# A decoder megakernel: the order of work at three places (geometry's transposed maxima, the scan's gate, inputs and norms, products at the end of the int8 stage)

## The chip, the cores and the metric

The kernel runs on one core of one Trainium2 chip. The metric is the device time of the whole launch in microseconds. Engines are named as the profile names them: PE is TensorE (PEld its weight loads), DVE VectorE, ACT ScalarE, POOL GpSimd, SP SyncE, which issues the DMAs.

## The reference, cut to what matters

Twelve layers follow each other, each in the form `x = layernorm(x + layer(x))`, on an input of 8 batches of 256 tokens of 256 values, in float32. Three of them are touched.

Layer 0, an attention with 16 heads whose keys and values get a part that a geometric memory has gated:

```
L = p1[_PI] * p2[_PJ] - p1[_PJ] * p2[_PI];  L / norm(L)      # lines of four projections
k_enh = k + kv_gate * gram_gate * k_geo
v_enh = v + kv_gate * gram_gate * v_geo
scores = einsum('bhtd,bhsd->bhts', q, k_enh) * SCALE         # causal
out = softmax(scores) @ v_enh;  out @ out_w + out_b
```

Layer 8, a product of numbers rounded to int8:

```
q_lhs = clip(round(lhs / lhs_scale), -127, 127)   # lhs_scale: absmax of a row / 127
q_rhs = clip(round(rhs / rhs_scale), -127, 127)
return (q_lhs @ q_rhs) * lhs_scale * rhs_scale
```

Layer 9, a gated selective scan with 512 channels and 16 states:

```
gate = sigmoid(x @ W_gate.T + b_gate)
x_proj, delta_proj = split(x @ W_in.T + b_in);  delta = relu(delta_proj)
h = h * exp(A * d_t[..., None]) + (x_t * d_t)[..., None] * B_mat      # over 256 tokens
y_t = h @ c0
return gate * (y + x_proj * D_vec) @ W_out.T + b_out
```

## The kernel before

Each layer is a stage, a function that writes an instruction list for each engine by hand. There is no scheduler: what stands first in an engine's list runs first, and the engines meet at semaphores that count upwards (`M.max_done`, `M.prod_done` and so on). PSUM is eight banks: `R` (four), `T` (two) and `O` (two).

**geometry16 (layer 0).** The loop runs over rounds i = -2 to 11; batches pass through it in a pipeline, so that round i holds the scores of batch i (`scores`, queries by keys, L1624 and L1628, three parts f = 0, 1, 2), the scores by key of batch i-1 (`scores_t`, L1651, L1656), its products with the values (L1673, L1677), older outputs, and the features of batch i+2 (`features`, transposes, L1586). VectorE takes from the scores the negated maxima of the rows (`maxima`, `neg_max`, L1939). TensorE transposes these (`maxima_transposed`, L1637) into the bank `S_y`, ScalarE copies them to `neg_t` (L1836), and SyncE's DMA (L1495) writes them into a row of `q_pad`, so that `scores_t` of the same batch, in the next round, subtracts the maximum inside its product. `scores` and `scores_t` use the four banks of `R` in turn: a part is written when the maxima or the exponentials (L1832) before have been read. The bank `S_y` is shared, in the order of the table `MIXED_JOBS`, by the features, the maxima (`neg`), the memory (`mem`, L1595) and others; `mixed_free` waits until the job before has been read out. The three features of a round are read out by VectorE (`scanned`, L1907 a scan over tokens, L1910 a product). `maxima_transposed(i)` stands at the end of round i, behind `features(i, 2)`, and `scores(i + 1, 0)` begins the next. The rounds that have features are -2 to 5; `neg` is there in rounds 0 to 7, so that six rounds have both. The text counts these as first to sixth.

**int8_product (layer 8).** VectorE quantises rows of batch i, TensorE transposes them (L2993) and multiplies (L3003), VectorE adds the residual and normalises batch i-3 (L3099), TensorE transposes the result (`transposed`, L3013) for the next stage and ScalarE copies it to `x_t` (L3051). `keep_warm` (L212) is a 128x512 product into a part of PSUM that nothing reads; it stands once in each round but the last four, which have no rows left to transpose.

**selective_scan (layer 9).** The work is cut into 16 units i: four pairs of batches g, each with four blocks of 128 channels ct. A unit has 16 states n. ScalarE computes the decays (L3349, into a ring of 6), VectorE scans (`scanned`, L3418, into a ring of 10), TensorE adds two states at a time into `R` (`summed`, L3255). For the next unit TensorE projects `delta`, `x` and gate (L3224) and ScalarE reads them (L3335, L3339 to `xp`, L3343); VectorE forms `u = xp * delta` (`weighted`, L3411). When a unit's sums are complete, ScalarE copies the odd half (`odd`), TensorE adds it swapped (`swapped`, L3261), VectorE multiplies with the gate (`product`, L3424), and TensorE projects the output (`output`, L3276). After the fourth block of a pair, in the first unit of the next pair (`leaving`, three such units), VectorE adds the residual and takes statistics (`residual`, L3429), GpSimd computes the reciprocal deviation (`rstd`, L3490 and L3492), VectorE normalises (`normalised`, L3442), TensorE transposes (`transposed`, L3285) and ScalarE copies (L3364), for each of the pair's two batches. The numbers n in the code say behind which scan, pair of sums or decay each of these stands.

## Time and profile before

| | us |
|---|---|
| the three runs | 3420.35, 3420.55, 3434.16 |
| their median | 3420.55 |
| the profiled execution | 3430.85 |
| its span, first to last instruction | 3429.0 |
| TensorE busy, 90% of the span | 3095.6 |
| VectorE busy, 48% | 1661.0 |
| ScalarE busy, 36% | 1221.8 |
| geometry's stage, from the start of the span | about 388 |
| int8's stage | about 2640 to 2682 |
| the scan's stage | about 2682 to 3038 |

The profile is of one execution, whose times are counted from its first instruction. A row of it names the engine, the line, the tile written and those read; "idle before" is the time that the engine stood still just before the row's first instruction, with what ended it. TensorE's instructions are pipelined: the next one starts before the recorded end of the one before it. The granted clock is given as a share of 2.4 GHz, so that 0.50 is the lower level of 1.2 GHz.

### The profile page before, as it was taken

Reading aid. Unit: us, or ns where it says so; the run is one execution under the profiler, and the core shown is the slowest. Engines: PE = TensorE matmul, PEld = TensorE weight load, DVE = VectorE, ACT = ScalarE, POOL = GpSimd, SP = SyncE. Lnnn points to the kernel's source line nnn. Section 1 sums busy time; section 2 is a strip of 40 time slices with the busy share of each in tenths; the row PEclk is TensorE's granted clock in tenths of the full one; section 3 lists DMA queues with packets and bytes.
Section 4 is the critical chain, followed back from the end, with each engine's and each line's share of the span. In section 5 each row is a group of like instructions: output and inputs, shape, how many; then the busy total and the mean of one; then the engine's idle time right before and its main releaser. Section 6 shows DMA issues by size and latency. Waiting matters only on the chain. (4 is left out here: it accounts for less than half of the span.)

```text
span 3429.0 us, 56123 instructions
## 1 busy us (share of the span) xinstructions
PE 3095.6 (90%) x22948; PEld 1968.3 (57%) x22948; DVE 1661.0 (48%) x2939; ACT 1221.8 (36%) x2636; POOL 291.0 (8%) x511
## 2 busy tenths in 40 slices
PE   6999899999989998899999988989998888889695
PEld 4565466666658886656666655656555333346363
DVE  4565344444433323634444443225557899956112
ACT  1322254445431112234544441123332666633011
POOL 1111100000000000000000000000111000001202
PEclk9999999999999999899999999989999999989897
DMA  2001000000100002000000000010000000000332
GB/s 103 18 13 61 9 1 1 1 1 1 59 16 0 0 0 79 20 1 1 1 1 1 1 26 28 12 33 21 10 28 34 16 1 1 1 19 14 148 129 85
DMA packets 36410, 85.14 MB, mean 25 GB/s; under 512 B 3246, under 2 KB 30103, under 8 KB 32599
## 3 DMA queue, kind: packets, MB, share of 16 engines
q1 hardware_dynamic: 31831, 75.06, 6.3%
q0 software_dynamic: 1536, 4.20, 0.4%
q8 instruction: 170, 2.79, 0.3%
q10 hardware_dynamic: 2816, 2.62, 0.2%
q14 instruction: 57, 0.47, 0.0%
HBM read 53.90 MB, written 9.44 MB: 18 GB/s over the span
## 5 line engine op out<-in xcount | busy, mean ns | idle before, releaser
L2329 ACT ACTIVATE prob<-R,neg_max 128x333 f32<-128x333 f32 x512 | 268.6, 538 | 183.1 <-DVE neg_max L2399 183.1
L3418 DVE TENSOR_TENSOR_SCAN arena<-arena,u 128x512 f32<-128x512 f32 x256 | 289.6, 1204 | 0.1
L2399 DVE TENSOR_REDUCE neg_max<-R 128x2 f32<-128x666 f32 x256 | 205.6, 845 | 98.1 <-PE R L2209 98.1
L2220 PEld LDWEIGHTS T<-const,prob 128*128 128x128 f32 (+1 forms) x1536 | 183.6, 143 | 96.2 <-issue 66.1
L2405 DVE COPY prob_t<-T 128x384 f32<-128x384 f32 x256 | 141.7, 553 | 189.0 <-PE T L2220 183.8
L2220 PE MATMUL T<-const,prob 128*128 128x128 f32 (+1 forms) x1536 | 210.5, 273 | 19.7 <-DVE prob_t L2405 19.5
L2336 ACT ACTIVATE prob_t<-T 128x384 f32<-128x384 f32 x256 | 126.1, 493 | 213.9 <-PE T L2220 207.2
L3349 ACT ACTIVATE arena<-delta,neg_a 128x510 f32<-128x510 f32 x256 | 176.5, 714 | 53.4 <-DVE arena L3418 52.7
L2169 PE MATMUL O<-arena,keys_in 128*128 128x512 f32 (+1 forms) x384 | 183.8, 603 | 5.0 <-ACT arena L2310 2.4
L2164 PE MATMUL O<-keys_in,arena 128*128 128x333 f32 x512 | 170.3, 458 | 1.2 <-DVE arena L2380 1.2
L3255 PE MATMUL R<-arena,diag 64*64 64x512 f32 x1024 | 138.6, 635 | 33.2 <-DVE arena L3418 32.9
L2648 PE MATMUL R<-x_t,arena 128*128 (+1 forms) x640 | 152.1, 382 | 1.0 <-PEq L2644 0.6
L2512 POOL COPY rec_rows<-rec 128x256 f32<-128x256 f32 x128 | 51.2, 400 | 1001.5 <-DVE rec L2410 1001.5
L2648 PEld LDWEIGHTS R<-x_t,arena 128*128 128x128 f32 x640 | 121.7, 191 | 20.1 <-issue 3.2
L2158 PE MATMUL O<-keys_in,arena 128*128 128x256 f32 x512 | 124.4, 387 | 3.2 <-ACT keys_in L2304 2.4
L2657 PE MATMUL O<-arena,hid 128*128 128x256 f32 x512 | 121.3, 380 | 2.3 <-PEq L2654 2.3
L2180 PE MATMUL O<-arena,attn_t 128*128 128x256 f32 x512 | 117.4, 382 | 1.0 <-DVE ysb L2382 1.0
L2770 DVE SCALAR_TENSOR_TENSOR ysb<-O,gate_b,ysb 128x256 f32<-128x256 f32 x112 | 49.1, 480 | 142.8 <-DVEq L2767 142.8
L2416 DVE TENSOR_TENSOR attn_t<-O,arena 128x256 f32<-128x256 f32 x128 | 53.8, 420 | 130.4 <-ACT arena L2341 130.4
L2164 PEld LDWEIGHTS O<-keys_in,arena 128*128 128x128 f32 x512 | 88.1, 190 | 40.9 <-DVE arena L2380 7.4
L2657 PEld LDWEIGHTS O<-arena,hid 128*128 128x128 f32 x512 | 97.1, 190 | 16.0 <-issue 2.6
L2158 PEld LDWEIGHTS O<-keys_in,arena 128*128 128x128 f32 x512 | 92.2, 189 | 22.0 <-ACT q_t L2307 4.2
(463 smaller groups left out, 5497.0 us busy)
## 6 DMA issues: line engine op xcount, KB each, us to landing
w<-w_dram SPq DMA_DIRECT2D x16, 1024.0 KB, 7.5
arena<-pack_dram SPq DMA_DIRECT2D x2, 4100.0 KB, 15.0
q_pad<-q_pad SPq DMA_DIRECT2D x24, 224.0 KB, 2.7
arena<-pack_dram SPq DMA_DIRECT2D x4, 1284.0 KB, 6.0
arena<-pack_dram SPq DMA_DIRECT2D x1, 4896.0 KB, 15.1
arena<-k_nat SPq DMA_DIRECT2D x16, 224.0 KB, 2.7
arena<-arena SPq DMA_DIRECT2D x16, 224.0 KB, 2.9
arena<-pack_dram SPq DMA_DIRECT2D x1, 2707.0 KB, 14.9
```

The costliest lines, as they stand in the source:

```text
L2158: last = nc.tensor.matmul(bank[:, h * T:(h + 1) * T], wq[:, c, (2 * i + h) * P:(2 * i + h + 1) * P], keys[:, c, CTX:XK], start=(c == 0), s ...
L2164: last = nc.tensor.matmul(bank[:, 0:XK], wkv[:, c, i * P:(i + 1) * P], keys[:, c, :], start=(c == 0), stop=(c == C - 1))
L2169: last = nc.tensor.matmul(bank[0:n, :], keys[:, c, first:first + n], wkv[:, c, XI + i % 2 * BANK:XI + (i % 2 + 1) * BANK], start=(c == 0), ...
L2220: last = nc.tensor.transpose(S.T[0:n, i, kc * P:(kc + 1) * P], prob[:, g % 2, i, first:first + n], S.ident)
L2329: last = nc.scalar.activation(prob[:, g % 2, i, :], S.R[:, g % 2, i * BANK:i * BANK + XK], ACT.Exp, bias=neg_max[:, g % 2, i:i + 1], accum ...
L2399: nc.vector.tensor_reduce(neg_max[:, g % 2, :], S.R[:, g % 2, :].rearrange("p (i n) -> p i n", i=2)[:, :, 0:XK], AX.X, ALU.max, negate=Tru ...
L2405: nc.vector.tensor_copy(prob_t[:, m % 2, 0, :, qt * P:(qt + 1) * P], S.T[:, 0, 0:3 * P].rearrange("p (c q) -> p c q", c=3)).then_inc(M.pt_ ...
L2648: last = nc.tensor.matmul(S.R[:, e % 2, f * T:(f + 1) * T], w[:, f * P:(f + 1) * P], S.x_t[:, c, bass.ds(b * T, T)], start=(c == 0), stop= ...
L2657: last = nc.tensor.matmul(S.O[:, slot, tt * D:(tt + 1) * D], src[:, f * T + tt * P:f * T + (tt + 1) * P], w[:, f, :], start=(f == 0), stop ...
L3255: last = nc.tensor.matmul(sums(i, a)[to:to + HB, :], diag[rows, i % CT, n + a, :], state[rows, (q + a) % HELD, :], start=(a == 1 and n == ...
L3349: nc.scalar.activation(decay[:, q % DEEP, :].rearrange("p (b t) -> p b t", b=PAIR)[:, :, 1:T], delta[:, i % 2, :].rearrange("p (b t) -> p ...
L3418: nc.vector.tensor_tensor_scan(state[:, q % HELD, :], decay[:, q % DEEP, :], u[:, i % 2, :], 0.0, ALU.mult, ALU.add)\
```

## The change

- geometry: `maxima_transposed(i)` goes from the end of round i to the next round, behind `scores(i + 1, 0)`. `neg_max` gets two copies that alternate by batch.
- int8: each of the last three rounds gets one unread product (L212) ahead of its transposes.
- scan, VectorE: the product with the gate goes from behind scan 6 to behind scan 7, `weighted` from 8 to 9, the first residual from 11 to 12, the first norm and the second residual from 13 to 15, and the second norm from 15 to scan 2 of the next unit. TensorE: the transposes of the second batch go from behind the first pair of sums to behind the third. ScalarE: their copy goes from decay 8 to decay 12.

```diff
@@ geometry16
-        neg_max = sb("neg_max", [P, TT, H])
+        neg_max = sb("neg_max", [P, 2, TT, H])
...
                 if now:
                     scores(i, 0)
+                if before:
+                    maxima_transposed(i - 1)
                 written(i, 0)
...
                 features(i, 2)
-                if now:
-                    maxima_transposed(i)
...
@@ int8_product, tensor
                     keep_warm(nc, S, unread, 1)
+                if i >= B:
+                    keep_warm(nc, S, unread, 1)
                 if 0 <= i - 3 < B:
                     transposed(i - 3)
...
@@ selective_scan, tensor
                     summed(i, n)
+                    if n == 4 and g >= 1 and ct == 1:
+                        transposed(PAIR * g - 1)
                     if n == 0:
-                        if g >= 1 and ct == 1:
-                            transposed(PAIR * g - 1)
                         if i + 1 < UNITS:
                             deltas(i + 1)
...
@@ selective_scan, scalar
-                    if n == 8 and g >= 1 and ct == 1:
+                    if n == 12 and g >= 1 and ct == 1:
                         transposed(PAIR * g - 1)
...
@@ selective_scan, vector
-                    if n == 6 and i >= 1:
+                    if n == 7 and i >= 1:
                         product(i - 1)
-                    if n == 8 and i + 1 < UNITS:
+                    if n == 9 and i + 1 < UNITS:
                         weighted(i + 1)
-                    if n == 11 and leaving:
+                    if n == 12 and leaving:
                         residual(PAIR * g - 2)
-                    if n == 13 and leaving:
+                    if n == 15 and leaving:
                         normalised(PAIR * g - 2)
                         residual(PAIR * g - 1)
-                    if n == 15 and leaving:
+                    if n == 2 and g >= 1 and ct == 1:
                         normalised(PAIR * g - 1)
```

TensorE's list between round 0 and round 1 of geometry: L1637 transposes the maxima, L1624 and L1628 are the scores of the next batch, L1535 the first projection of its round.

```order
@@ -52,7 +52,7 @@
 L1573 MATMUL T<-arena,x_t 128x512 x2
 L1586 MATMUL T<-const,arena 112x128 x4
-L1637 MATMUL T<-const,neg_max 16x128 x2
 L1624 MATMUL R<-k_pad,q_pad 128x128 x16
 L1628 MATMUL R<-masks,ident_b 128x512 x4
+L1637 MATMUL T<-const,neg_max 16x128 x2
 L1535 MATMUL T<-arena,x_t 128x192 x2
 L1538 MATMUL T<-arena,x_t 128x192 x2
```

The transposed maxima went behind the 20 products of the next scores; nothing else changed its place.

VectorE's list in the scan, from the residual of the first leaving unit to the gate product of the unit behind it, before. L3418 are the scans.

```order
L3429 TENSOR_TENSOR ysb_own<-O,x_nat 128x512
L3433 BN_STATS bst<-ysb_own 128x6 x2
L3436 BN_AGGR mv<-bst 128x2 x2
L3418 SCALAR_TENSOR_TENSOR arena<-arena,u 128x512 x2
L3442 TENSOR_SCALAR x_nat<-ysb_own,mv,rstd 128x256 x2
L3429 TENSOR_TENSOR ysb_own<-O,x_nat 128x512
L3433 BN_STATS bst<-ysb_own 128x6 x2
L3436 BN_AGGR mv<-bst 128x2 x2
L3418 SCALAR_TENSOR_TENSOR arena<-arena,u 128x512 x2
L3442 TENSOR_SCALAR x_nat<-ysb_own,mv,rstd 128x256 x2
L3418 SCALAR_TENSOR_TENSOR arena<-arena,u 128x512 x7
L3424 SCALAR_TENSOR_TENSOR gated<-gated,R 128x512
```

The same piece of VectorE's list after the change. The lines of this stage are two further down in the changed file, so that L3420 are the scans and L3426 the gate product.

```order
L3431 TENSOR_TENSOR ysb_own<-O,x_nat 128x512
L3435 BN_STATS bst<-ysb_own 128x6 x2
L3438 BN_AGGR mv<-bst 128x2 x2
L3420 SCALAR_TENSOR_TENSOR arena<-arena,u 128x512 x3
L3444 TENSOR_SCALAR x_nat<-ysb_own,mv,rstd 128x256 x2
L3431 TENSOR_TENSOR ysb_own<-O,x_nat 128x512
L3435 BN_STATS bst<-ysb_own 128x6 x2
L3438 BN_AGGR mv<-bst 128x2 x2
L3420 SCALAR_TENSOR_TENSOR arena<-arena,u 128x512 x3
L3444 TENSOR_SCALAR x_nat<-ysb_own,mv,rstd 128x256 x2
L3420 SCALAR_TENSOR_TENSOR arena<-arena,u 128x512 x5
L3426 SCALAR_TENSOR_TENSOR gated<-gated,R 128x512
```

Three scans stand between each statistics and its norm where there were two; the boundary of the units, which lay behind the second norm, now lies behind the second statistics.

## Rows read from the trace of the kernel before

**Rows 1.** Which engine is busy in the scan stage: stretch, then its length, busy us, clock, DMA.

```profile
2682.00:3038.00 356.00, 310.22 (x1472) 109.63 (x1472) 327.89 (x355) 224.74 (x378) 16.87 (x16) 0.93 0.01 4
```

**Rows 2.** Time order, geometry, end of a round: start, us, engine, line, shapes, idle before.

```profile
207.87 0.60 PE L1586 MATMUL T<-const,arena 128*112 128x128 f32 x4
...
209.84 0.38 PE L1637 MATMUL T<-const,neg_max 128*16 128x128 f32 x2 [1.36 <-DVE arena L1910]
...
210.14 1.17 PE L1624 MATMUL R<-k_pad,q_pad 16*128 16x128 f32 x32
...
210.25 0.37 ACT L1836 ACTIVATE neg_t<-T 16x256 f32<-16x256 f32 x1 [1.58 <-PE T L1637]
...
212.12 0.82 PE L1535 MATMUL T<-arena,x_t 128*128 128x192 f32 x4
```

**Rows 3.** Time order, TensorE, the same place in the fifth and sixth round.

```profile
248.72 0.38 PE L1637 MATMUL T<-const,neg_max 128*16 128x128 f32 x2 [1.72 <-DVE arena L1910]
...
288.88 0.38 PE L1637 MATMUL T<-const,neg_max 128*16 128x128 f32 x2 [1.37 <-DVE arena L1910]
```

**Rows 4.** Busy time by stretch, behind two of those gaps (columns as in rows 1).

```profile
133.00:136.00 3.00, 3.00 (x40) 2.11 (x39) 0.18 (x1) 0.37 (x1) 0.00 (x0) 0.77 0.04 11
...
136.00:139.00 3.00, 3.00 (x39) 2.64 (x41) 2.11 (x1) 0.49 (x1) 0.00 (x0) 0.66 0.00 0
...
252.00:255.00 3.00, 3.00 (x43) 2.56 (x45) 1.85 (x1) 0.49 (x1) 0.00 (x0) 0.65 0.00 0
```

**Rows 5.** Time order, TensorE: scores by key, sixth round and eighth.

```profile
294.58 1.15 PE L1651 MATMUL R<-q_pad,k_pad 17*128 17x256 f32 x16
...
355.89 1.15 PE L1651 MATMUL R<-q_pad,k_pad 17*128 17x256 f32 x16 [0.22 <-DMA q_pad<-neg_t]
```

**Rows 6.** Instructions of tile neg_t: its DMA, duration ns min/median/max, first and last start.

```profile
L1495 SPq DMA_DIRECT2D q_pad<-neg_t x8: 572/594/698, 99.0 to 354.0; - x8
```

**Rows 7.** Time order, TensorE, end of int8 and the scan's first projections.

```profile
2673.03 1.02 PE L212 MATMUL R<-ctx_t,const 128*128 128x512 f32 x2
...
2680.30 0.66 PE L3013 MATMUL R<-const,x_nat 128*128 128x128 f32 x4 [0.46 <-DVE x_nat L3099]
...
2682.07 8.24 PE L3224 MATMUL T<-x_t,arena 128*128 128x512 f32 x12 [1.11 <-PEq L2962]
```

**Rows 8.** Busy time by stretch, before the scan stage (columns as in rows 1).

```profile
2681.00:2681.50 0.50, 0.00 (x0) 0.00 (x0) 0.00 (x0) 0.50 (x1) 0.00 (x0) 0.50 0.00 0
```

**Rows 9.** Time order, scan: the first xp on ScalarE, a projection on TensorE at 1.00.

```profile
2688.63 0.69 ACT L3339 ACTIVATE xp<-T,arena 128x512 f32<-128x512 f32 x1 [2.08 <-PE T L3224]
...
2798.68 1.88 PE L3224 MATMUL T<-x_t,arena 128*128 128x512 f32 x4
```

**Rows 10.** Time order, VectorE in the scan stage, where it idles.

```profile
2689.42 0.69 DVE L3411 TENSOR_TENSOR u<-xp,delta 128x512 f32<-128x512 f32 x1 [4.36 <-ACT xp L3339]
...
2701.54 0.69 DVE L3411 TENSOR_TENSOR u<-xp,delta 128x512 f32<-128x512 f32 x1 [1.19 <-ACT xp L3339]
...
2782.61 0.69 DVE L3429 TENSOR_TENSOR ysb_own<-O,x_nat 128x512 f32<-128x512 f32 x1 [0.57 <-PE O L3276]
...
2787.22 0.73 DVE L3442 TENSOR_SCALAR x_nat<-ysb_own,mv,rstd 128x256 f32<-128x256 f32 x2 [0.54 <-POOL rstd L3492]
...
2802.68 0.69 DVE L3424 SCALAR_TENSOR_TENSOR gated<-gated,R 128x512 f32<-128x512 f32 x1 [1.65 <-PE R L3261]
...
2806.12 15.72 DVE L3418 TENSOR_TENSOR_SCAN arena<-arena,u 128x512 f32<-128x512 f32 x14
...
2822.18 0.69 DVE L3424 SCALAR_TENSOR_TENSOR gated<-gated,R 128x512 f32<-128x512 f32 x1 [0.34 <-PE R L3261]
...
2963.18 0.74 DVE L3442 TENSOR_SCALAR x_nat<-ysb_own,mv,rstd 128x256 f32<-128x256 f32 x2 [0.55 <-POOL rstd L3492]
...
2973.36 0.69 DVE L3424 SCALAR_TENSOR_TENSOR gated<-gated,R 128x512 f32<-128x512 f32 x1 [1.62 <-PE R L3261]
```

**Rows 11.** Busy time by stretch, first leaving unit (columns as in rows 1).

```profile
2790.00:2792.00 2.00, 0.02 (x3) 0.02 (x3) 1.93 (x2) 0.76 (x2) 1.85 (x2) 0.50 0.00 0
```

More of the change, by code:

```diff
@@ L1636, in maxima_transposed @@
                 for qt in range(TT):
-                    last = nc.tensor.transpose(S_y[0:H, qt * P:(qt + 1) * P], neg_max[:, qt, :], S.ident)
+                    last = nc.tensor.transpose(S_y[0:H, qt * P:(qt + 1) * P], neg_max[:, b % 2, qt, :], S.ident)
                 last.then_inc(M.ya_full, 1)
@@ L1937, in maxima @@
                 n = P if f == 0 else T
-                neg = neg_max[:, min(f, 1), :].rearrange("p (j c) -> p j c", j=4)
+                neg = neg_max[:, b % 2, min(f, 1), :].rearrange("p (j c) -> p j c", j=4)
                 nc.vector.tensor_reduce(neg if f == 0 else neg[:, :, 2 * f - 2:2 * f],
```

## The prediction

> **What bounds the kernel now.** I read the busy time by stage first, then the order of events at the three places that the edit touches, engine by engine, and there only what ends last. The kernel as a whole is TensorE's, but the three places differ. In geometry's loop TensorE is the bound. Its queue runs dry once in each of the six rounds that carry features: behind the last four transposes of the features (L1586) stands the transpose of the maxima (L1637), which waits until VectorE has read those features out of the same PSUM bank (L1910), 1.36 us of idle time; behind L1637 stand the scores (L1624), which wait for nothing [rows 2]. In the scan stage VectorE is the bound: it is busy 327.9 of 356 us, TensorE 310.2 [rows 1], and between two VectorE instructions of a unit there is no gap but the ones that the trace names [rows 10]. At the end of the int8 stage the bound is the chain VectorE norm, TensorE transpose, ScalarE copy; behind it TensorE starts the scan's first projections at the lower of its two clock levels, 1.2 GHz (granted clock 0.50) [rows 7, 8], and the first scan waits for them.
>
> **Geometry: 8.6 us, and part of the clock.** The scores go ahead of the transposed maxima. They last 212.12 less 210.14, or 1.98 us [rows 2], longer than the 1.36 that TensorE waits, so L1637 then finds its bank read out. Five gaps of 1.36 to 1.37 and one, the fifth, of 1.72 [rows 2, 3] give 8.6. Bounds: from the start of L1586 to that of L1535 are 4.25 us, of which after the change 0.6 (L1586), 1.98 and 0.3 (L1637) are left, so 1.4 a round or 8.2 in all; if the transposes of L1586 overlap what follows as L1637 does, 1.6 a round or 9.6. What is moved back: L1637 starts about 0.5 us later on the clock, and 1.9 later against TensorE's work, and with it ScalarE's neg_t, SyncE's DMA into q_pad and the scores by key (L1651) that wait for it. ScalarE's in-order queue has neg_t at its head and waits next for L1535's product, which comes behind L1637 again, so nothing is blocked there. The DMA lands in at most 1.9 us: the last one is issued at 354.0 and L1651 starts at 355.89, after 0.22 of waiting [rows 5, 6]. The tightest feature round is the sixth, where L1651 starts at 294.58, 5.7 us behind its L1637 at 288.88 [rows 3, 5]: the path of neg_t takes 0.41 to ScalarE, 0.37 there [rows 2] and 1.9, in sum 2.7, and the room that is left is 5.7 less 1.9 less 2.7, or 1.1. So no new wait; the cost if it fails is in the rivals. L1624 now meets its own waits (the DMAs of keys and queries, the exponentials of the round before) 1.7 us earlier; in rows 2 it starts straight behind L1637, so how much earlier it could start isn't shown, and the bounds for that are nothing and the whole 8.6. In the seventh round L1637 sat in a wait for ScalarE, and afterwards it costs its own 0.3. The second copy of neg_max adds no instruction.
>
> In two of the six rounds the gap is followed by about 6 us in which the granted clock averages 0.7, that is a stretch at 1.2 GHz and the rest at 2.4 [rows 4]. Lost: (1 - 0.77 + 1 - 0.66) x 3, or 1.7 us, and as much in the other, whose second half reads 0.65. Without the gap before it the drop should be gone: 3.4 in this execution. Below nothing: a drop that comes elsewhere costs as much. Since four like gaps have none behind them, I carry half, 1.7, to other executions. The Trainium skill (TensorE: Matmul & The Clock Gate, Part 1) says that the phase of the chip's look at activity isn't tied to the kernel, so that slow matmuls differ from run to run; two of six gaps agree with that. By that rule the drops are no property of the gap alone, and the whole gain would be 1.7 us smaller.
>
> **End of int8: 2.4 us.** Three unread products are added before the last three transposes. Each is like the present ones, 1.02 us of TensorE [rows 7]. The first two fall in idle time. The third stands between the last two transposes, where TensorE has 0.46 idle: the last transpose, its copy and the end of the stage come 0.1 to 0.6 later; I take 0.3, because the next instruction starts before the recorded end of the one before it (0.86 behind the start of this product). In exchange TensorE doesn't idle for most of the 5 us before the stage's end. In the trace the clock falls to 0.50 at about 2681 [rows 8], and the first scan's input waits for eight matmuls: from 2682.07 to ScalarE's xp at 2688.63, 6.56 us. Four such matmuls take 1.88 at 2.4 GHz [rows 9], eight then 3.8, and xp is 2.7 earlier. VectorE's own setup ends 4.36 us before the product of xp starts [rows 10], so it allows that. Net 2.4. Ends: -0.3 (the clock falls all the same) and 2.7.
>
> **Scan: 12.0 us.** All of it is idle time of VectorE. (1) The product with the gate moves one scan later, n = 6 to 7. A scan is 15.72 / 14, or 1.12 us [rows 10]. In the first unit after each leaving pair it waits 1.65 (the last of the three: 1.62) for TensorE's swapped sums, in the next unit 0.34 [rows 10]. One scan would cover 1.12 of the first; the other 0.53 goes because more VectorE work now stands ahead of it: the first batch's norm (0.73) and the second's residual (0.69 and its statistics) [rows 10] come behind the last scan of the old unit, where they came before it. (2) The input product moves from n = 8 to 9: in unit 0 it waits 1.19 for xp, and 0.07 stays: 1.1. (3) Each norm now has three scans (3.36) between itself and its residual rather than two. It waited 0.54 for GpSimd after two, so 1.12 more covers it: six times 0.54. (4) The residual is one scan later and no longer waits 0.57 for the output product: three times. Sum of a leaving pair: 1.65 + 0.34 + 1.08 + 0.57 = 3.64; three of them 10.9; with (2) 12.0. Each unit's last product, outputs and norms after the last scan aren't touched.
>
> What is moved past what: TensorE's transposes of the second batch go from behind the first to behind the third pair of sums, ScalarE's copy from its decay 8 to 12. The decays run up to six scans ahead of VectorE, so the copy is wanted at about scan 7, and the output product that reuses its bank stands behind the fifth pair, which needs scan 9. A wait of ScalarE for the transposes there is covered by the decays in hand. TensorE: in the leaving unit it is busy 0.02 of the 2 us from 2790 to 2792, at a granted clock of 0.50 [rows 11]; there a norm and a residual stand between the fourteenth and the fifteenth scan. In the new order only the first residual is left among a unit's last scans, so I expect it to drop less. It has little room in the unit behind: 310.2 us over 16 units is 19.4 each [rows 1], against 16 scans of 1.12 and two products of 0.69 on VectorE, 19.3, or 20.0 with a norm.
>
> **Sum.** 8.6 - 0.3 + 3.4 + 2.4 + 12.0 = 26.1 us, or 3404.7 from the profiled execution's own 3430.85. That one is 10.3 above the median of 3420.55, beside 3434.16, and drops of the clock like the two above may be part of it. On the median I take 26.1 - 1.7 = 24.4: 3396.
>
> **Rivals.** (A) As above, 0.55. (B) The clock doesn't follow: the scan still opens at 1.2 GHz (-2.7) and the drops only move (-1.7): 3400.5; for it speaks that 1.11 us without any product stay between the stages [rows 7]; 0.15. (C) In geometry the DMA of the maxima takes the removed wait's place: it would have to land 1.1 us later than now, and takes back at most the 8.3: 3404; 0.05. (D) VectorE's pause now falls at the start of the unit in which TensorE has most to do. If its clock drops there rather than in the idle half, the three projections (1.88 each at 2.4 GHz [rows 9]) take 5.6 us longer, the swapped sums and xp are late, and three times 5.6, 17 us, come back: 3413; against it, the pauses of VectorE are spread over two units; 0.12. (E) The other side: the same, but TensorE stays at 1.2 GHz through that whole unit, 39 us against VectorE's 20.0: 3 x 19 less 24 is 33 slower, 3453. It decides once more than 8.1 us are lost in each, which is 16 us in a row at 1.2 GHz; in the trace it is back at 2.4 by 2798.68 [rows 9], 7 us after the stretch of rows 11: 0.03. (F) The executions fall where 3434.16 fell, 13.6 higher, with the gain intact: 3410; 0.10.
>
> **Numbers.** 3396 is A's, with a range of its own from 3388 to 3403 (its ends: 9.6 and 8.2 in geometry, clock 0 or 3.4, int8 0 to 2.7, 1.5 us of scan waits left). For 8 in 10 the range runs to F and D: 3387 to 3412. A change under 0.5% (17.1 us) can't be told from none here; that is above 3403.4. Faster: A nearly whole, most of B, little else: 0.70. Slower by as much: E and a piece of F: 0.04. Same: 0.26.
>
> **What would show it.** Right: L1637 without idle time before it and L1535 some 1.5 us nearer to L1586; a granted clock of 1.00 at the scan's first projections and their twelve matmuls in 5.7 rather than 8.24 us; no waits of VectorE in the units 1 to 14 for gate, rstd or output. Wrong: idle time of L1651 for its DMA; the gate product waiting in the unit behind a leaving one with TensorE at 0.50; or all three as forecast and a total that hasn't moved, which would mean that the stages between lost on the clock what these gained.

## The result

| Kernel | Median, us | Lowest to highest, us | Executions | Profiled execution, its span, us | Granted clock |
|---|---|---|---|---|---|
| before | 3420.85 | 3420.35 to 3434.16 | 4 | 3430.85, 3429.0 | 0.960 |
| changed | 3389.51 | 3381.86 to 3401.92 | 4 | 3394.49, 3392.7 | 0.967 |

The ratio of the changed kernel to the one before is 0.990, 95% interval 0.9865 to 0.9935: faster by 31 us by the medians (22 to 46 by the interval). By the ratio itself it is 34 us, or about 3387. The prediction was 24.4 us, 3396. A second comparison of the same two kernels (below) gave 0.9911, 0.9884 to 0.9938, which is 30 us. The direction and the places were right, the size was forecast too small.

To see where the time went I cut each trace at the first instruction of a stage. Stage lengths in us:

| Trace | start and geometry (layer 0) | layers 1 to 6 | layer 7 and int8 (8) | scan (9) | layers 10 and 11 |
|---|---|---|---|---|---|
| before | 388.5 | 2111.5 | 182.1 | 356.3 | 390.6 |
| changed | 373.1 | 2107.2 | 182.2 | 339.4 | 390.8 |
| difference | -15.4 | -4.3 | +0.1 | -16.9 | +0.2 |

The 4.3 us in layers 1 to 6 aren't the change's: the same code took from 2096.6 to 2111.5 us there in ten traces.

From the page of the changed kernel, its span and its busy time by engine:

```profile
span 3392.7 us, 56135 instructions
PE 3077.6 (91%) x22954; PEld 1959.4 (58%) x22954; DVE 1659.0 (49%) x2939; ACT 1222.0 (36%) x2636; POOL 291.9 (9%) x511
```

Geometry first: the changed kernel in order of time at the end of the same round as [rows 2] (start, us, engine, line, shapes, idle before and who ended it).

```profile
202.03 0.60 PE L1586 MATMUL T<-const,arena 128*112 128x128 f32 x4
...
202.56 1.17 PE L1624 MATMUL R<-k_pad,q_pad 16*128 16x128 f32 x32
...
204.54 0.38 PE L1637 MATMUL T<-const,neg_max 128*16 128x128 f32 x2
...
204.76 0.82 PE L1535 MATMUL T<-arena,x_t 128*128 128x192 f32 x4
...
204.96 0.37 ACT L1836 ACTIVATE neg_t<-T 16x256 f32<-16x256 f32 x1 [2.13 <-PE T L1637]
```

The maxima's transpose (L1637) has no idle time before it, and from the start of L1586 to that of L1535 are 2.73 us instead of 4.25. A whole round says the same. These are the four products at L1573, which the change doesn't touch and which come once in a round, in the first two of the six rounds of before:

```profile
94.32 1.98 PE L1573 MATMUL T<-arena,x_t 128*128 128x512 f32 x4 [0.35 <-DVE arena L1882]
...
129.04 1.99 PE L1573 MATMUL T<-arena,x_t 128*128 128x512 f32 x4 [0.35 <-DVE arena L1882]
```

and in the same two rounds of the changed kernel:

```profile
94.73 1.99 PE L1573 MATMUL T<-arena,x_t 128*128 128x512 f32 x4 [0.35 <-DVE arena L1882]
...
127.92 1.98 PE L1573 MATMUL T<-arena,x_t 128*128 128x512 f32 x4 [0.35 <-DVE arena L1882]
```

The round takes 33.19 us where it took 34.72, which is 1.53 less, although the wait that went was recorded as 1.37. The fifth round, whose wait was recorded as 1.72, is 1.8 shorter once its drop of the clock is taken off. The clock, in busy time by stretch (stretch, its length, busy us of PE, PEld, DVE, ACT, POOL with instructions, granted clock, DMA share, GB/s), in before:

```profile
130.00:168.00 38.00, 35.63 (x358) 22.98 (x357) 22.37 (x30) 12.03 (x17) 3.87 (x6) 0.96 0.05 14
...
278.00:310.00 32.00, 27.75 (x287) 17.52 (x285) 18.19 (x28) 8.25 (x10) 2.19 (x6) 0.89 0.03 9
310.00:340.00 30.00, 27.83 (x295) 15.38 (x295) 10.99 (x7) 7.63 (x11) 1.20 (x2) 0.94 0.40 157
```

and in the changed kernel, whose rounds come up to 11 us earlier by then:

```profile
130.00:168.00 38.00, 36.99 (x402) 23.79 (x400) 24.15 (x33) 12.63 (x19) 3.88 (x6) 1.00 0.05 14
...
278.00:310.00 32.00, 27.74 (x386) 18.46 (x388) 18.79 (x25) 9.73 (x13) 2.14 (x4) 0.95 0.22 80
310.00:340.00 30.00, 26.81 (x296) 14.98 (x284) 11.45 (x12) 6.38 (x5) 2.13 (x4) 1.00 0.18 74
```

From 94 to 278 us the clock of the changed kernel is 1.00 throughout. Before, it was 0.96 and 0.95 in two of these rounds, the drops of [rows 4].

The end of int8 and the opening of the scan, TensorE and VectorE in order of time in the changed kernel, against [rows 7, 10], and the clock against [rows 8]:

```profile
2659.43 0.66 PE L3013 MATMUL R<-const,x_nat 128*128 128x128 f32 x4 [0.37 <-DVE x_nat L3101]
...
2659.92 1.02 PE L212 MATMUL R<-ctx_t,const 128*128 128x512 f32 x2
...
2660.78 0.60 PE L3013 MATMUL R<-const,x_nat 128*128 128x128 f32 x4
...
2662.50 5.39 PE L3226 MATMUL T<-x_t,arena 128*128 128x512 f32 x12 [1.11 <-PEq L2962]
...
2667.01 0.69 DVE L3413 TENSOR_TENSOR u<-xp,delta 128x512 f32<-128x512 f32 x1 [1.50 <-ACT xp L3341]
```

```profile
2661.00:2661.50 0.50, 0.39 (x4) 0.14 (x2) 0.00 (x0) 0.08 (x1) 0.00 (x0) 1.00 0.00 0
```

The twelve projections take 5.39 us where they took 8.24, and VectorE waits 1.50 us for xp where it waited 4.36.

The scan stage against [rows 1], and all that VectorE still waits for in it beyond the opening, 0.12 us for xp in unit 0 and 0.42 us of issue at 2928.15, against [rows 10]:

```profile
2662.00:3001.00 339.00, 301.95 (x1472) 107.52 (x1472) 326.12 (x355) 223.66 (x379) 16.86 (x16) 0.97 0.01 5
```

```profile
2990.20 0.69 DVE L3426 SCALAR_TENSOR_TENSOR gated<-gated,R 128x512 f32<-128x512 f32 x1 [3.80 <-PE R L3263]
2992.12 0.69 DVE L3431 TENSOR_TENSOR ysb_own<-O,x_nat 128x512 f32<-128x512 f32 x1 [1.22 <-PE O L3278]
2995.16 0.74 DVE L3444 TENSOR_SCALAR x_nat<-ysb_own,mv,rstd 128x256 f32<-128x256 f32 x2 [1.21 <-POOL rstd L3494]
2998.85 0.73 DVE L3444 TENSOR_SCALAR x_nat<-ysb_own,mv,rstd 128x256 f32<-128x256 f32 x2 [1.21 <-POOL rstd L3494]
```

VectorE has the same 355 instructions and works almost without a wait (0.12 and 0.42 us) through all sixteen units' scans; it is 96% busy where it was 92%. (From the int8 stage on, line numbers of the changed kernel are up to 2 higher.) What is left waits behind the last scan, which nothing was moved to cover.

### The profile page after: what moved, and what is told of

Read it like the earlier page. It is cut to its first block and busy times, and to the rows that moved or that the text cites. A ratio compares the mean times of both kernels' runs of the same rounds, so it can differ in the third digit from the quotient of the medians.

```text
span 3392.7 us, 56135 instructions
## 1 busy us (share of the span) xinstructions
PE 3077.6 (91%) x22954; PEld 1959.4 (58%) x22954; DVE 1659.0 (49%) x2939; ACT 1222.0 (36%) x2636; POOL 291.9 (9%) x511
## 2 busy tenths in 40 slices
DMA packets 36410, 85.14 MB, mean 25 GB/s; under 512 B 3246, under 2 KB 30103, under 8 KB 32599
## 5 line engine op out<-in xcount | busy, mean ns | idle before, releaser
L3420 DVE TENSOR_TENSOR_SCAN arena<-arena,u 128x512 f32<-128x512 f32 x256 | 289.5, 1201 | 0.1
L3257 PE MATMUL R<-arena,diag 64*64 64x512 f32 x1024 | 136.1, 622 | 24.6 <-DVE arena L3420 24.4
L2164 PEld LDWEIGHTS O<-keys_in,arena 128*128 128x128 f32 x512 | 88.2, 190 | 40.9 <-DVE arena L2380 7.4
L212 PE MATMUL R<-ctx_t,const 128*128 128x512 f32 x162 | 82.5, 639 | 29.1 <-DMA slots_in<-x_nat,to 26.4
```

The costliest lines, as they stand in the source:

```text
L2164: last = nc.tensor.matmul(bank[:, 0:XK], wkv[:, c, i * P:(i + 1) * P], keys[:, c, :], start=(c == 0), stop=(c == C - 1))
L3257: last = nc.tensor.matmul(sums(i, a)[to:to + HB, :], diag[rows, i % CT, n + a, :], state[rows, (q + a) % HELD, :], start=(a == 1 and n == ...
L3420: nc.vector.tensor_tensor_scan(state[:, q % HELD, :], decay[:, q % DEEP, :], u[:, i % 2, :], 0.0, ALU.mult, ALU.add)\
```

## The experiments

The theory: the gain is the sum of three independent pieces, each the idle time of the engine that bounds its stage, with the lower clock that followed it. The rivals: the pieces are worth something else when each stands alone; in geometry it is the clock and not the idle time that pays; in the scan one half of the moves does all. "Stretch" below is the time in geometry from the first L1573 to the start of the next stage. It leaves out the program's opening, in which the clock comes up at slightly different times.

**Geometry's part alone.**

```diff
-        neg_max = sb("neg_max", [P, TT, H])
+        neg_max = sb("neg_max", [P, 2, TT, H])
...
+                if before:
+                    maxima_transposed(i - 1)
...
-                if now:
-                    maxima_transposed(i)
```

> Geometry's part alone. Theory: the three parts are independent, and geometry's brings most of what the forecast missed: 1.5 us a round by the starts of the instructions (9.2 in six rounds, less 0.3 in the seventh) and 3 to 6 us of clock drops that go with the gaps, in sum 12 to 15 us less than before, about 3407. Rival 1 (the forecast's sum): 8.3 of gaps and half of 3.4 of clock, 10 less, about 3411. Rival 2 (luck in stages that nobody touched makes the difference): the rounds of this kernel spread as widely as those of before, over 14 us, and the geometry stage itself ends about 10 us earlier than before, not 15.

Measured: 0.9956 (0.9938 to 0.9974), or 15 us by that ratio; geometry's stage 376.7 us against 388.5, the stretch 331.3 against 343.8. This trace keeps one more drop of the clock than that of the changed kernel:

```profile
278.00:310.00 32.00, 27.74 (x301) 17.11 (x301) 17.48 (x25) 9.36 (x12) 2.13 (x4) 0.84 0.11 32
```

As an estimate, work at half the clock takes twice as long (eight of the scan's sums took 1.98 us in such a stretch and 1.09 at the full clock, somewhat less than twice), so that (1 - granted clock) times the stretch is what a drop costs. From 94 to 340 us before loses 8.6 us by this (1.5 + 1.8 + 3.5 + 1.8 in four stretches), this kernel 5.1, the changed kernel 1.6. With five gaps at 1.53 and the fifth at 1.8 (9.4 in sum) and 0.3 in the seventh round, that gives 9.4 - 0.3 + 3.5 = 12.6 here, where 12.5 was measured, and 9.4 - 0.3 + 7.0 = 16.1 for the changed kernel, where 15.8 was.

**The unread products at int8's end alone.**

```diff
+                if i >= B:
+                    keep_warm(nc, S, unread, 1)
```

> The three unread products at int8's end alone. Theory: the scan's first twelve matmuls run at 2.4 GHz (5.4 us rather than 8.2), the stage ends 0.3 us later, 2.4 us less in all, about 3418.5. Rival: the clock at the scan's opening isn't set by these products but by where the executions happen to lie: the twelve matmuls take 8.2 us again and the time is 0.3 more.

Measured: 0.9992 (0.9975 to 1.0008), which the comparison can't tell from nothing; the trace can. The twelve projections take 5.39 us, VectorE waits 1.51 instead of 4.36, the scan stage is 352.9 us instead of 356.3, and the stage before it 182.0 instead of 182.1. Of these 3.4 us only the 2.85 at the opening are the edit's. The other 0.5 lies in the three gate products behind the leaving units, which wait 1.37, 1.62 and 1.56 here instead of 1.65, 1.75 and 1.62, and the kernel with geometry's part alone, whose scan and int8 stages are those of before, shows the same (1.36, 1.61, 1.55), the first at

```profile
2783.91 0.69 DVE L3424 SCALAR_TENSOR_TENSOR gated<-gated,R 128x512 f32<-128x512 f32 x1 [1.36 <-PE R L3261]
```

The rival, that the opening's clock is a matter of where an execution happens to lie, falls over all traces: in the six kernels without these products (before, geometry's part, the filled gaps, the scan's part and each of its halves) the granted clock of the scan's first 5.4 us is 0.50 to 0.58, in the four with two or three of them 1.00.

**The scan's moves alone.**

```diff
+                    if n == 4 and g >= 1 and ct == 1:
+                        transposed(PAIR * g - 1)
...
-                    if n == 6 and i >= 1:
+                    if n == 7 and i >= 1:
                         product(i - 1)
-                    if n == 8 and i + 1 < UNITS:
+                    if n == 9 and i + 1 < UNITS:
                         weighted(i + 1)
-                    if n == 11 and leaving:
+                    if n == 12 and leaving:
...
-                    if n == 13 and leaving:
+                    if n == 15 and leaving:
...
-                    if n == 15 and leaving:
+                    if n == 2 and g >= 1 and ct == 1:
                         normalised(PAIR * g - 1)
```

> The scan's moves alone (gate product, input product, residuals, norms, the transposes behind them). Theory: every wait of VectorE between units goes, each worth its recorded idle time and about 0.08 us more that the next instruction gains by starting before the end of the one before it: 12.0 and 1.5 to 2, in sum 13.5 to 14 less, about 3407; the first twelve matmuls still take 8.2 us. Rival (the forecast's sum): 12.0 less, 3409.

Measured: 0.9961 (0.9943 to 0.9979), 13 us. The scan stage is 342.9 us, 13.4 less; geometry's 389.0 and the last two layers' 390.6 are as before. Of all the waits of [rows 10] the opening (4.44) is left, and beside it one of 0.68 for the gate, late in the stage, which the whole change doesn't show, and those behind the last scan.

**The whole change again,** beside its parts on the same chip.

> The whole change once more, beside its parts. Theory: the sum of the three parts, 28 to 31 us less than before, about 3391, with a spread of some 10 to 20 us between executions. Rival: the parts interact (the int8 part worth more or less once the scan is changed, or clock drops that the earlier start moves elsewhere), and the whole differs from the sum by more than 5 us.

Measured: 0.9911 (0.9884 to 0.9938), 30 us by the ratio. The three parts give 0.44%, 0.08% and 0.39%, together 0.91% against 0.89%. So they add as far as the intervals, each about 0.2% to either side, can tell. Geometry's stretch is 331.3 us here, as in the kernel with geometry's part alone, and the scan stage 339.4.

**Geometry's gaps filled, order as before.** Two unread products stand ahead of the maxima's transpose in the six feature rounds. TensorE starts them when its queue would have gone idle, and no idle time is won.

```diff
+                if now and i < B - AHEAD:
+                    if i == 0:
+                        pe.wait_ge(M.max_done, 3)
+                    else:
+                        pe.wait_ge(M.exp_done, 3 * i)
+                    keep_warm(nc, S, bank(0), 2)
                 if now:
                     maxima_transposed(i)
```

> Geometry in its old order, with two unread 128x512 products of 0.86 us each in front of the transposed maxima in the six rounds that have the gap. They fill the gap but win none of it: what this kernel gains is the clock's share alone. Theory (the removed gaps bring 9 us by themselves and about 3 by clock drops that go with them): the granted clock of the feature rounds is 1.00 throughout and the time is 3.4 to 6 less for that, 1.2 more for the products being a little longer than the gap, so 2 to 5 less than before, about 3418. Rival (the drops come from elsewhere and only happened to follow two of the gaps): they are still there in one or two rounds, and the time is 1 us more than before.

Measured: 0.9976 (0.9958 to 0.9994), 8 us by the ratio. Its stage length, 378.8, looks as good as the reorder's, but 4 us of that lie before the first round. In order of time on TensorE, the first L1573 stands at 40.5 us where before has it at 44.7: ahead of it some groups of products ran at half the pace in before and not in this execution (four of 512 columns at 31.69 took 3.78 us, here at 28.98 they took 1.99), though the edit touches nothing there. The stretch is what counts: 338.3 us, 5.5 less than before, against 12.5 less for the reorder. At the end of a round TensorE shows

```profile
202.58 0.60 PE L1586 MATMUL T<-const,arena 128*112 128x128 f32 x4
203.02 1.88 PE L212 MATMUL R<-ctx_t,const 128*128 128x512 f32 x4
204.74 0.38 PE L1637 MATMUL T<-const,neg_max 128*16 128x128 f32 x2
```

The gap has become work of 1.88 us. L1637 follows L1586 by 2.16 us where before had 1.97 (209.84 less 207.87 in [rows 2]), so a round pays 0.2 us more, about 1.2 in six. The clock is the changed kernel's:

```profile
130.00:168.00 38.00, 37.00 (x385) 23.21 (x378) 22.76 (x30) 12.02 (x17) 3.86 (x6) 1.00 0.05 14
...
278.00:310.00 32.00, 28.59 (x333) 18.23 (x333) 19.63 (x29) 8.07 (x12) 2.13 (x4) 0.95 0.03 9
310.00:340.00 30.00, 26.72 (x284) 14.82 (x286) 12.73 (x11) 6.37 (x5) 2.13 (x4) 1.00 0.37 149
```

Lost to the clock: 1.6 us instead of 8.6, so 7.0 - 1.2 = 5.8 against the 5.5 measured. This takes geometry's gain apart: 3.5 to 7 us are the clock, and the gaps themselves are the other 9. Of the 7.0 here 3.4 are the drops behind the second and the fifth gap of before. The rest lies behind the last gap, where three of the four kernels in the new order lose as much as before (5.1 us), so that one trace of this kernel doesn't show it to be the products' doing.

**The scan's two halves.** First the two products alone:

```diff
-                    if n == 6 and i >= 1:
+                    if n == 7 and i >= 1:
                         product(i - 1)
-                    if n == 8 and i + 1 < UNITS:
+                    if n == 9 and i + 1 < UNITS:
                         weighted(i + 1)
```

> Of the scan's moves only the gate product (6 to 7) and the input product (8 to 9). The forecast's split: 1.12 of the 1.65 in three units, 0.34 in three more, 1.1 in unit 0, 5.5 in sum, and the waits for rstd (0.54) and for the output (0.57) stay; the gate product keeps 0.5 of its wait in the unit behind a leaving one. With the overlap that a wait costs on top, 6 less than before, about 3415. Rival: no wait is left but those for rstd and output, since TensorE also comes sooner.

Measured: 0.9978 (0.9958 to 0.9998). The scan stage is 355.1 us, only 1.2 less, and not even that is the edit's: 0.6 comes from the opening, where VectorE waits 3.77 instead of 4.36. From the first u to the end of the stage are 348.3 us, against 348.9 in before and 348.4 in the kernel with geometry's part alone, which leaves 0.1 to 0.6. VectorE in order of time, in the unit behind the first leaving one and in the next:

```profile
2796.07 0.69 DVE L3424 SCALAR_TENSOR_TENSOR gated<-gated,R 128x512 f32<-128x512 f32 x1 [0.86 <-PE R L3261]
...
2817.26 0.69 DVE L3424 SCALAR_TENSOR_TENSOR gated<-gated,R 128x512 f32<-128x512 f32 x1 [2.03 <-PE R L3261]
```

The first wait fell from 1.65 to 0.86, and the second rose from 0.34 to 2.03. Between the two the clock of TensorE fell, which it didn't do at this point before:

```profile
2801.00:2805.00 4.00, 4.00 (x20) 2.12 (x19) 4.00 (x4) 3.42 (x6) 0.00 (x0) 0.94 0.00 0
2805.00:2809.00 4.00, 4.00 (x20) 2.37 (x22) 4.00 (x5) 2.38 (x4) 0.00 (x0) 0.63 0.01 4
```

In the second of the three groups it doesn't fall, and the waits are 0.56 and 0.35, where before has 1.75 and 0.34; in the third it falls, and they are 0.97 and 1.99. So one scan covers what it should (1.19 us, forecast 1.12) where the clock stays up, and the fall takes it back in the other two. What makes the clock fall there isn't shown; the kernel of the next experiment, which leaves the gate product in its place, has the fall and a wait of 1.79 at the first group too. The comparison's interval, a gain of 1 to 14 us, reaches nearly down to that. The rest of this trace's shorter span isn't the edit's: layers 1 to 6, which are the same code, took 2103.0 us against 2111.5, and layer 7 with int8, also the same, 185.5 against 182.1.

Then the rest of the moves alone, norms, residuals, transposes and ScalarE's copy:

```diff
+                    if n == 4 and g >= 1 and ct == 1:
+                        transposed(PAIR * g - 1)
...
-                    if n == 8 and g >= 1 and ct == 1:
+                    if n == 12 and g >= 1 and ct == 1:
...
-                    if n == 11 and leaving:
+                    if n == 12 and leaving:
...
-                    if n == 13 and leaving:
+                    if n == 15 and leaving:
...
-                    if n == 15 and leaving:
+                    if n == 2 and g >= 1 and ct == 1:
```

> Of the scan's moves only residuals, norms and the transposes behind them; the gate product stays at 6. The forecast's split: six times 0.54, three times 0.57 and 0.53 of each 1.65, 6.6 in sum, with a wait of about 1.1 left for the gate product behind the leaving unit. Rival (the moved norm work alone already covers the gate product): no wait is left there either, the gain is 10 to 12, and the two halves of the scan's edit overlap, so that they don't add up to the whole's 13.4.

Measured: 0.9963 (0.9942 to 0.9985); the scan stage is 346.8 us, 9.5 less. No wait for rstd or for the output product is left. The wait for xp in unit 0 and some for the gate remain, the longest being the second of these:

```profile
2699.22 0.69 DVE L3411 TENSOR_TENSOR u<-xp,delta 128x512 f32<-128x512 f32 x1 [1.19 <-ACT xp L3339]
2817.60 0.69 DVE L3424 SCALAR_TENSOR_TENSOR gated<-gated,R 128x512 f32<-128x512 f32 x1 [1.79 <-PE R L3261]
```

The gate waits ahead of the last come to 3.8 us (0.17, 1.79, 0.15, 0.60, 1.09), against 6.2 in before (1.65, 1.75, 1.62, three of 0.34 and one of 0.14). So at most 0.6 and 9.5 alone, 13.4 together: some 3 us come only when both are made. The product's later place is worth little while VectorE still pauses in the leaving unit, since what it frees there is taken back in two of three groups by the next unit.

**More unread products.** To the changed kernel are added five in the last scan unit (after sums 0, 4, 6, 10 and 12) and five around the last transposes, and the third of the int8 stage is left out.

```diff
-                if i >= B:
+                if i in (B, B + 1):
                     keep_warm(nc, S, unread, 1)
...
+                    if i == UNITS - 1 and n in (0, 4, 6, 10, 12):
+                        keep_warm(nc, S, S_x, 1)
...
+            keep_warm(nc, S, S_x, 3)
...
+            keep_warm(nc, S, S_x, 2)
```

> The changed kernel, with unread products also in the scan's last unit (five, where TensorE has no projections left and idles 1.1 us a pair), three and two around the last transposes, and the third one at int8's end taken out. Theory: TensorE stays at 2.4 GHz to the scan's end; its last output and sums take 1.9 and 2.8 rather than 3.8 and 2.9, VectorE's last wait falls from 3.8 to about 2.5, the next stage's first eight matmuls take 1.9 rather than 3.75; in sum 3 us less than the changed kernel. int8's end comes 0.25 us sooner and its clock still holds. Rival: those last matmuls don't lie on the path, or the clock falls all the same, and nothing changes.

Measured: 0.9895 (0.9867 to 0.9924) to the kernel before, within the changed kernel's own intervals. The scan stage is 340.0 us against 339.4, the stages behind it 390.5 against 390.8. The clock did as meant, in the changed kernel

```profile
2992.00:3000.00 8.00, 2.42 (x11) 1.57 (x10) 4.76 (x14) 0.60 (x1) 1.87 (x4) 0.74 0.00 1
```

and in this one

```profile
2992.00:3000.00 8.00, 6.95 (x22) 3.65 (x22) 4.59 (x13) 0.60 (x1) 1.39 (x4) 1.00 0.00 1
3000.00:3008.00 8.00, 5.55 (x16) 3.75 (x17) 5.35 (x7) 1.44 (x3) 4.37 (x6) 0.79 0.00 0
```

but it fell again in the next 8 us, and VectorE's order of time shows what little the higher clock changed: the last gate product (L3430 in this file) waits 3.47 us (3.80 in the changed kernel), from its start to the end of the stage are 11.2 us (11.6), and two units whose waits had gone show one again.

```profile
2715.80 0.69 DVE L3430 SCALAR_TENSOR_TENSOR gated<-gated,R 128x512 f32<-128x512 f32 x1 [0.68 <-PE R L3263]
...
2797.52 0.69 DVE L3430 SCALAR_TENSOR_TENSOR gated<-gated,R 128x512 f32<-128x512 f32 x1 [0.68 <-PE R L3263]
...
2991.87 0.69 DVE L3430 SCALAR_TENSOR_TENSOR gated<-gated,R 128x512 f32<-128x512 f32 x1 [3.47 <-PE R L3263]
```

The tail behind the last scan is a chain of hand-overs between engines, and the clock sets little of it, some 0.8 us. In this one trace the scan opens at the full clock with two products as with three (VectorE waits 1.51), and the int8 stage is 0.2 us shorter, so the third doesn't seem to be needed. This kernel is no better than the changed one.

## Why the prediction was right in kind and too small

The forecast named the right three places, the right mechanism at each and about the right proportions. What failed is the size of its terms, in two steps of the sum. The drops of the clock behind geometry's gaps, 3.4 us in the profiled execution, were halved to 1.7 for other executions; every trace with the gaps has the whole 3.4. And each removed wait was priced at its recorded idle time, which leaves out 0.08 to 0.16 us a time: 0.8 us in geometry and 1.4 in the scan. A third part, up to 3.5 us of clock later in geometry, stood in no term, and whether it belongs to the change is open.

| Term | Forecast, us | Traces, us |
|---|---|---|
| geometry's six gaps | 8.6 | 9.4 |
| seventh round | -0.3 | -0.3 kept, fits the stretches |
| geometry's clock | 3.4 profiled, 1.7 carried on | 3.5 in three traces, 7.0 in one |
| int8 and the scan's opening | 2.4 | 2.7 |
| scan | 12.0 | 13.4 alone, 14.1 in the whole |
| sum | 26.1 profiled, 24.4 on the median | 28.7 to 32.9 |

The forecast's own upper ends (9.6 - 0.3 + 3.4 + 2.7 + 12.0) add up to 27.4, or 3393; the 3388 that it gives as the end of this range doesn't follow from them, and what the traces show, 28.7 to 32.9, lies above it. Both comparisons measured more than 27.4 too (34 and 30 us by the ratios).

**The gaps.** The step "five gaps of 1.36 to 1.37 and one of 1.72 give 8.6" took the recorded idle time as the price of the wait. Four rounds shrank by 1.52 or 1.53 each and the fifth by 1.8; the sixth is taken like the four. Behind a wait the first instruction also starts without the overlap with its forerunner that it has in a stream: before, L1637 was followed by L1624 after 0.30 us; now L1637, in the stream, is followed by L1535 after 0.22, and L1624 starts 0.53 behind L1586, of which 0.60 is recorded. The prediction had nearly this as its upper bound (1.6 a round, 9.6) and took 8.6, near its lower bound of 8.2.

**The clock.** The forecast that the drops go with the gaps was right; halving them for other executions was wrong. Five traces have the old order with its gaps (before, and the kernels with int8's part, the scan's or one of its halves). In each of them exactly two drops begin 1.3 to 2.1 us behind the start of an L1637 that had waited, and cost 1.7 us apiece. In before and in the kernel with the scan's part these are the second and the fifth gap, in the other three the fourth and the sixth, as here in the kernel with int8's part, where L1637 starts at 208.80 and 287.84:

```profile
211.00:214.00 3.00, 3.00 (x14) 2.48 (x16) 2.29 (x1) 0.00 (x0) 0.00 (x0) 0.50 0.01 2
289.50:292.50 3.00, 3.00 (x36) 1.73 (x38) 1.45 (x1) 0.00 (x0) 0.00 (x0) 0.50 0.04 11
```

In the four traces with the new order and in that of the filled gaps no drop begins within 7 us behind any of these six transposes. This agrees with what the Trainium skill (TensorE: Matmul & The Clock Gate, Part 1) says of the phase, that it isn't tied to the kernel. But from "the drop moves" it doesn't follow that "the loss is chance": which gaps are hit changes, how many doesn't. Behind the last gap there are more drops, which I hadn't looked at. They cost 3.4 to 5.1 us in the five traces with gaps, 5.1 in three of those with the new order, and 1.7 in the fourth, the changed kernel's first trace, and in that of the filled gaps. That is why that first trace gained 7.0 and not 3.5; why it did isn't settled, and only the 3.4 behind the gaps is shown to go with the change. The lengths agree: the five stretches with gaps are 342.1 to 343.9 us, those with the new order 331.2, 331.3 and 331.3 and, in that first trace, 328.0.

**Int8 and the opening.** The step "I take 0.3" for the third product was right, if a little high: the last transpose follows the one before by 1.35 us (2659.43 to 2660.78) instead of 1.12 (2679.18 to 2680.30), 0.2 more, and the whole stage is 182.2 us against 182.1. From the scan's first product to u are 4.51 us instead of 7.35, so the opening gained 2.84, forecast 2.7.

**The scan.** The waits named went, but for 0.12 of the 1.19 in unit 0 (0.07 was forecast to stay). A leaving pair was forecast at 1.65 + 0.34 + 1.08 + 0.57 = 3.64; from one pair's gate product to the same product of the next are, before, 85.14 us,

```profile
2775.16 0.67 DVE L3424 SCALAR_TENSOR_TENSOR gated<-gated,R 128x512 f32<-128x512 f32 x1
...
2860.30 0.67 DVE L3424 SCALAR_TENSOR_TENSOR gated<-gated,R 128x512 f32<-128x512 f32 x1
```

and in the changed kernel 81.09 (2752.55 to 2833.64), or 4.05 less. Three pairs and unit 0's 1.19 give the 13.4 of the scan's part alone; in the whole change the late wait of 0.68 is missing as well, so that from the first u to the end of the stage are 334.8 us instead of 348.9, 14.1 less. Five waits went in a pair, so each is worth 0.08 us more than its recorded idle time: in the stream VectorE starts an instruction 0.08 before the recorded end of the last (2.33 us of scans from 2753.13, the next instruction at 2755.38), behind a wait it can't. The split of the gate's wait (1.12 for the later product) held in the group where the clock stayed up, 1.19; in the other two the later product alone covered 0.79 and 0.65, and the next unit waited 2.0.

**The rivals.** B, that the clock doesn't follow, fell: 1.00 at the scan's opening and behind all six of geometry's former gaps. C, the DMA of the maxima, fell: all waits for it at L1651 come to 0.7 us in both kernels. D and E, TensorE slow at the start of the unit behind the leaving one, were right about the place and wrong about the size (forecast 17 us lost and more). The clock does fall there, twice in three times; the first,

```profile
2764.54 1.98 PE L3257 MATMUL R<-arena,diag 64*64 64x512 f32 x8 [1.14 <-DVE arena L3420]
...
2767.82 2.05 PE L3247 MATMUL R<-xp,skip 128*128 128x512 f32 x2 [0.26 <-issue]
...
2771.16 1.98 PE L3226 MATMUL T<-x_t,arena 128*128 128x512 f32 x4
```

(eight sums take 1.09 at the full clock), but it is back by the first projection, and the gate product one scan later absorbs the delay. F, that the executions fall at 3410 with the gain intact, didn't happen: the highest of the changed kernel's ten in both comparisons is 3402.56.

## What to carry to other kernels

Price a removed wait by the distance between two instructions that stay, not by the idle time printed at the wait: the latter leaves out the lost overlap, 0.08 us on VectorE and 0.16 on TensorE at five of the six gaps here. When idle time goes in a stage that TensorE bounds, count the slow stretches that follow it, and carry them in full if several executions show as many of them, be it in other rounds; keep those apart that don't begin at a wait. And test moves that share one engine's slack together: here one half was worth at most 0.6, the other 9.5, and both 13.4 us.

## What the runs showed of the hardware that I had not expected

The same code in layers 1 to 6 took from 2096.6 to 2111.5 us in ten traces. That is half of the spread between executions of the kernel before (3406.4 to 3434.3 us in one set of 28, 3409.9 to 3441.1 in another). These stages are TensorE's, and their busy time moves with their length: the trace of before, then that of the filled gaps,

```profile
388.50:2500.00 2111.50, 1985.59 (x14542) 1341.89 (x14542) 878.96 (x1820) 763.73 (x1940) 136.73 (x293) 0.97 0.04 13
```

```profile
378.80:2475.40 2096.60, 1971.39 (x14543) 1332.77 (x14541) 878.41 (x1821) 762.77 (x1940) 136.66 (x293) 0.98 0.04 13
```

14.2 of the 14.9 us are TensorE's busy time, at 0.98 against 0.97 of the clock. An edit worth 3 us, such as the int8 products, can't be seen in totals beside that, only in the lengths of the stages that it touches.

That unread products in gaps of 1.4 us keep the clock from falling behind them, for about 1.2 us of added time, is the other. They returned 7 us in their one trace, of which the 3.4 behind the gaps are shown to be theirs. Filling the gaps brought 5.5 us where removing them brought 12.5 to 15.8.
